# A scatter by GpSimd made to follow the projections of a spiking attention and mixture-of-experts layer, step by step

## The reference

```python
xn = layernorm(x)
# attention: spikes are 0/1, lif(v, th) = (v >= th)
Q = lif(layer_norm(xn @ Wq.T + bq, gq, betaq), 1.0)   # K and V likewise, 16 heads of 16
attn = Dh - hamming(Q, K) + log_position_bias          # no softmax
out = lif((attn * scale) @ V, 0.5)
attention = lif(layer_norm(out @ Wo.T + bo, go, betao), 1.0)
# experts: 8 experts, the two best for each token
probs = softmax(xn @ router_w.T); scores, idx = top_k(probs, 2); scores /= scores.sum()
hidden_e = silu(h_e[:, :256]) * h_e[:, 256:],  h_e = xn @ up_proj[e]
experts = sum over the two chosen e of score_e * (hidden_e @ down_proj[e])
```

## Time and profile before

| What | Value |
|---|---|
| Three runs, median | 511.02 us (509.71, 511.02, 511.58) |
| The profiled execution, span from first to last instruction | 510.6 us |
| TensorE busy in it | 384.5 us, 75% |
| VectorE, ScalarE, GpSimd busy | 273.3, 232.6, 211.0 us |
| Mean granted TensorE clock | 0.883 |
| Bytes moved | 58.98 MB, mean 116 GB/s |

### The profile page before, as it was taken

The page is one execution under the profiler, slowest core; times in us unless marked ns, Lnnn a source line. Parts: engine busy times, 40 slices in busy tenths (PEclk is TensorE's granted clock), DMA queues, the critical chain, the costliest instruction groups (busy, mean ns, idle before and its releaser), DMA issues.

```text
span 510.6 us, 9171 instructions
## 1 busy us (share of the span) xinstructions
PE 384.5 (75%) x2517; PEld 312.9 (61%) x2526; DVE 273.3 (54%) x774; ACT 232.6 (46%) x752; POOL 211.0 (41%) x213
## 2 busy tenths in 40 slices
PE   5498773110113999998999999999999999999960
PEld 2234662100112999997778888888888887667650
DVE  5799971000100687996545444554455442458995
ACT  1567421000001788986545544454445543366650
POOL 5242467777771000000233333333333333259993
PEclk9799985555555799999999999999999999999995
DMA  8721223222220111320443344343443332495222
GB/s 269 247 96 41 83 83 125 104 104 104 104 105 31 42 41 41 106 83 1 144 131 121 121 119 136 118 124 113 124 134 123 118 98 74 184 369 193 100 84 83
DMA packets 40432, 58.98 MB, mean 116 GB/s; under 512 B 6294, under 2 KB 27926, under 8 KB 40408
## 3 DMA queue, kind: packets, MB, share of 16 engines
q1 hardware_dynamic: 31712, 38.53, 24.5%
q0 software_dynamic: 6848, 18.70, 10.1%
q10 hardware_dynamic: 1848, 1.47, 0.9%
HBM read 35.79 MB, written 22.89 MB: 115 GB/s over the span
## 4 chain that ended last, share of the span: by engine, by line
PE 54%; issue 21%; DVE 10%; POOL 7%; DMA 3%; ACT 2%; SPq 1%; POOLq 0%; DVEq 0%; ACTq 0%
PE bank L1108 15%; PE bank L1109 14%; PE bank L1110 14%; POOL xres L718 3%; PE bank L1186 3%; PE bank L1251 3%; POOL xres L711 3%; PE bank L1235 3%; DMA xn<-x 2%; DVE xn L787 2%; DVE xst L765 2%; POOL rstd L703 1%; DVE w_f L808 1%; PE bank L1174 1%; PE bank L1195 1%
## 5 line engine op out<-in xcount | busy, mean ns | idle before, releaser
L692 POOL DMA_INDIRECT slot_y<-ey,dest x71 | 68.5, 965 | 214.6 <-ACT ey L554 186.2
L500 ACT ACTIVATE junk<-bank 128x256 bf16<-128x256 f32 x96 | 35.7, 379 | 89.8 <-remote 71.7
L677 POOL DMA_INDIRECT slot_x<-xn,pos x64 | 61.6, 963 | 23.9 <-issue 19.2
L996 DVE TENSOR_TENSOR hid<-gact,bank 128x256 f32<-128x256 f32 x71 | 29.9, 421 | 76.6 <-ACT gact L538 51.0
L1108 PE MATMUL bank<-ew,exT_h 128*128 x142 | 62.6, 441 | 5.6 <-issue 4.3
L1110 PE MATMUL bank<-w_h,xT_l 128*128 128x256 f32 x192 | 56.9, 296 | 11.3 <-issue 11.2
L795 DVE TENSOR_TENSOR xT_l<-xT,xT_h 128x256 fp32r<-128x256 f32 x28 | 12.9, 460 | 98.1 <-issue 54.1
L1109 PE MATMUL bank<-w_l,xT_h 128*128 128x256 f32 x192 | 56.9, 296 | 11.2 <-issue 11.2
L1108 PE MATMUL bank<-w_h,xT_h 128*128 128x256 f32 x192 | 57.1, 297 | 10.5 <-issue 10.4
L538 ACT ACTIVATE gact<-bank 128x256 f32<-128x256 f32 x71 | 27.4, 386 | 63.8 <-PE bank L1110 63.8
L1110 PE MATMUL bank<-ew,exT_l 128*128 x142 | 55.9, 394 | 0.0
(11 more groups left out here) (193 smaller groups left out, 967.9 us busy)
## 6 DMA issues: line engine op xcount, KB each, us to landing
ex<-slot_x SPq DMA_DIRECT2D x71, 129.0 KB
y_tok<-slot_y SPq DMA_DIRECT2D x8, 1024.0 KB, 13.6
ew_f<-experts SPq DMA_DIRECT2D x24, 256.0 KB, 2.6
xres<-x SPq DMA_DIRECT2D x16, 256.0 KB, 2.8
out<-xres SPq DMA_DIRECT2D x16, 256.0 KB, 2.1
xn<-x SPq DMA_DIRECT2D x6, 512.0 KB, 11.7
slot_y<-ey,dest POOLq DMA_INDIRECT x71, 2.8
xn<-x SPq DMA_DIRECT2D x4, 256.0 KB, 3.8
```

The source lines that it names most:

```text
L500: nc.scalar.activation(junk[:, i, :], proj_ps[r][i], ACT.Square, accum_out=ssq[:, r, i:i + 1]).then_inc(s["ssq_done"], 1)
L677: pool.indirect_dma_start(slot_x, bass.IndirectOffsetOnAxis(ap=pos[:, k, t:t + 1], axis=0), xn[:, t, :], None).then_inc(s["scattered"], 16)
L692: pool.indirect_dma_start(slot_y, bass.IndirectOffsetOnAxis(ap=dest[:, m % 4:m % 4 + 1], axis=0), ey[:, m % 4, :], None).then_inc(y_out[m ...
L996: v.tensor_tensor(hid[:, m % 2, :], gact[:, m % 2, :], h_ps[m % 2][:, F:2 * F], ALU.mult).then_inc(s["hid_done"], 1)
```

## The change

POOL waits before the two scatters of tile t until `proj_done` is at 3(t+3), that is, until the projections of step t+2 are done. Tiles 30 and 31 have no wait of their own and follow tile 29, which waits for the last step, 31.

```diff
 LAG = 3
 LATE = 11
+LEAD = 3
 FAR_ROWS = 5
...
             pool.wait_ge(s["placed"], 1)
             for t in range(NT):
+                if t + LEAD <= NT:
+                    pool.wait_ge(s["proj_done"], G3 * (t + LEAD))
                 for k in range(TOPK):
                     pool.indirect_dma_start(slot_x, bass.IndirectOffsetOnAxis(ap=pos[:, k, t:t + 1], axis=0),
                                             xn[:, t, :], None).then_inc(s["scattered"], 16)
```

## The result

The changed kernel takes 453.88 us (median of 4 runs, 452.99 to 455.22), the kernel before, run beside it, 511.23 us. The ratio is 0.888, with a 95% interval of 0.885 to 0.890. The forecast was 446, with a range of 431 to 487.

The account below looks back on a forecast made before the run. TensorE sets the pace except in a hole from about 77 to 166 us, blamed on dense scatters. From 510.6, projections ending at 162 instead of 235.3, plus 9 for the tail, gave 446.3, said as 446, range 431 to 487 us.

Parts of the forecast that it names:

- The hole and its cause: TensorE nearly idle from about 77 to 166 us because dense scatters hold back its issue and signals; at most 86 to 87 us to gain.
- Why the change helps: The scatter stream stays nearly as dense but now stops when TensorE falls behind; the hole was possible because POOL never stopped.
- Loss in the steps: 26 projection steps after step 5, at 2.9 us plus a chosen 0.5 us loss each, 13 us; projections end at 162.
- The tail: Last scatters and the `ex` load after step 31 delay the experts: 10.4 us less about 1.5, set at +9, bounds +7 and +11.
- some of it comes back: Last q turns, spikes and k-v sums run in the wait for the first `ex`, returning about 1.5 us.
- The pads' wait of ScalarE: ScalarE's step 11 needs tile 6's pads, queued behind POOL's new wait: 1 to 2 us once, hidden if POOL keeps up.
- The signs: Expected trace: scatters spread to about 168, ScalarE's remote waits under 15 us, first `ex` turn 10 to 13 us after projections.
- short falls: TensorE's granted clock, PEclk, was to stay near 1.0 apart from brief drops.
- 1, exclusion: Scatter and projection exclude each other however issued: projections end at 231, total 515; chance 0.06 in full or nearly.
- 2, an aftermath of each pair: The held-back state outlasts each tile's two scatters, 10 us each: steps of 12.5 us, total 683; chance 0.05.
- 3, written-out instructions: The hole belongs to the written-out code of steps 5 to 7 and stays; only the tail is added: 520; chance 0.04.
- 4, scatters only while VectorE is idle: Scatters proceed only when VectorE is idle: 4.4 us each, steps of 8.9 us, total 589; chance 0.01.

Follow-up runs that it names:

- 21, then a pause: Kernel before, but tiles 7 and up wait for all projections, so 21 transfers run first and 50 after: 511.98 us, ratio 1.000.
- halves of 64 rows: Kernel before, with each row scatter of 128 rows made as two of 64 rows, result the same: 599.57 us, ratio 1.172.
- At 1.43 us: Kernel before, no wait for projections; GpSimd does one small memset, waited for, after each of 71 transfers: 495.87 us, ratio 0.968.
- the kernel with two memsets: Kernel before, no wait for projections; two small memsets, each waited for, after every transfer (pitch 1.65 us): 464.80 us, ratio 0.908.
- a lead of 5: Changed kernel with LEAD 5 in place of 3, so tile t's scatters wait for step t+4: 461.62 us, ratio 0.903.
- The kernel with the new order: Changed kernel with the last spikes, q turns and k-v sums ahead of the first expert tile on TensorE, VectorE, ScalarE: 452.68 us, ratio 0.885.

## Why the prediction came out as it did

**The hole and its cause (right, and now shown).** The reading was that a dense stream of transfers holds back what TensorE issues and signals. Spreading it out takes the hole away, stopping it ends the hole, and nearly twice as many transfers make it nearly twice as long. (Two slips in the reading don't touch this: the hole's slices start with a 3 that the reading left out, and the 71.7 us are the three waits before `junk`, 8.0, 34.9, and 28.8; the 8.3 before `qT` come on top.) The runs add the size of it. Take the time from the first transfer to TensorE's last gap that is put down to `issue`, and divide it by the number of transfers:

| kernel | transfers | pitch, us | from the first to the last such gap, us | per transfer |
|---|---|---|---|---|
| before | 71 | 1.27 | 65.5 to 165.3 | 1.41 |
| 21, then a pause | 21 | 1.27 | 65.5 to 95.05 | 1.41 |
| halves of 64 rows | 135 | 1.21 | 67.6 to 254.8 | 1.39 |

The three agree at about 1.4 us. It is tempting to read this as the time for which each transfer keeps something busy that TensorE needs too, so that at a pitch of 1.27 a backlog of 0.14 us is added with each. Two runs speak against that simple form. At 1.43 us no backlog should grow, and the hole was still there, with 216 matmuls in 90 us. And 50 transfers at 1.27 us with TensorE idle should have left 50 × 0.14 = 7 us, and left none. So the 1.4 us hold for transfers and TensorE's work together, and are no price of a transfer by itself: transfers and TensorE seem to share something, and when the transfers come every 1.27 to 1.43 us there is not enough left for TensorE, whose work is then late and outlasts them. This is argued from the two runs, not shown. At 1.65 no loss is seen. Bytes and rows don't enter, nor whether the steps are written out. What the shared thing is, the runs don't show.

**Why the change helps (half right).** I had written that the hole was possible because GpSimd never stopped. The tie to TensorE does stop it, 17 times, but the kernel with two memsets shows that no tie is needed, only distance; and with the tie the order is free, ahead or behind. With the wait the mean pitch came out at 1.51 us, with stops just where TensorE is late. An even pitch of 1.51 without the tie was not run, so how much is the pitch and how much the place of the stops stays open.

**Loss in the steps (right in the sum, partly by luck).** Forecast: projections' end at 162, that is 73.3 us earlier. Measured: 72.1. Step 5 ends at 73.6 in the trace of after too, and 26 steps to 163.2 are 3.45 us each, forecast 2.9 + 0.5 = 3.4. The two parts were off against each other: the undisturbed step is 2.74, the loss 0.7. My 2.9 was 70 us over 24 steps, with the recovery of step 8 in it, and the 0.5 was a choice between bounds that no row set. The loss is uneven. The steps 7 to 10 (76.8 to 99.0) take 22.2 us, 11.2 more than 4 × 2.74, and lose more than half of the 18 us in all. They lie beside the seven pads (76.5 to 93.3), which have no wait of their own. With a lead of 5 the pads move to 82.8 to 99.8, and there the slow steps are those from 82.7 to 107.1; the last of these, 8.8 us from 98.4 on, has ScalarE's wait for the pads in it. That the pads cause the rest fits both traces, and no run took them away.

**The tail (the mis-sized term).** Forecast: +9, from 10.4 gross less 1.5. Measured: +10.7 gross, right to 0.3, then nothing back and 2.0 more, +12.7 in all. The step that failed is "some of it comes back: the last q turns, spikes and k-v sums, which now lie between the first expert tiles, can run in the wait". VectorE's program has `exT_l` of the first expert tile ahead of the last `qk_spk`. It waits 13.28 us for it at 176.56 and does the spikes at 177.58, behind the wait and not in it. The kernel with the new order does them at 167.00 and gets 1.4 us back, close to that credit. A part of the rest may be the clock: after the idle time the granted clock is 0.63 on average in the 10 us from 175, where 0.5 is the level of 1.2 GHz, and the first four `ex` turns take 1.21 us from first to last in place of 0.61; how much of the 2.0 us that explains wasn't measured. Against the span, 446.3 forecast and 451.2 measured, 3.7 of the 4.9 us are this term and 1.2 the steps. Of the other 2.7 to the median, 1.8 are what a run's time has over its span, which the forecast left out, and 0.9 lie between the profiled execution and the median run.

**The pads' wait of ScalarE.** Set at 1 to 2 us or hidden. In the changed kernel no such wait shows among ScalarE's large ones. With a lead of 5 ScalarE stands idle for 5.7 us before 102.9, at the place of this wait, and with two memsets for 12.4 us.

**The signs (all but one came).** L680 spreads to 170.6 (forecast 168), with L1113 as its releaser; "remote" of ScalarE is 10.5 (under 15); the clock stays near 1 but for the dips; the `ex` turn comes 12.5 us after the last projection (10 to 13); the end is within 3 us of 273.8. PEclk falls to 0.84 at 77 to 99 us, longer than "short falls" said.

**The rivals.** 1, exclusion: refuted by 647 matmuls beside 59 transfers, and by 16.0 of 16 us in the kernel with two memsets. 2, an aftermath of each pair: there is an aftermath, but it grows with the number of transfers and with TensorE's work beside them, and none is left at a distance of 1.65. 3, written-out instructions: refuted by that same kernel, and by the held steps 8 to 14 at 1.43. 4, scatters only while VectorE is idle: the median is 961 ns with VectorE busy for 58 of 90 us, as it was with 4.4. But the median hides something: the mean rose from 963 to 994 ns, and eight of the 64 took 1.03 to 1.47 us. Apart from the first, at 65.0, all of these started while a VectorE instruction with both inputs in SBUF was running, and took longer by what was left of it, less 0.12 us:

```profile
102.28 0.68 DVE L940 TENSOR_TENSOR ew<-ew_f,ew 128x512 f32 x1
...
102.42 1.37 POOL L680 DMA_INDIRECT slot_x<-xn,pos  x1 [1.03 <-PE bank L1113]
```

```profile
151.76 0.68 DVE L940 TENSOR_TENSOR ew<-ew_f,ew 128x512 fp32r<-128x512 f32 x1
151.81 1.47 POOL L680 DMA_INDIRECT slot_x<-xn,pos  x1 [0.31 <-issue]
```

The transfers that started inside the spikes (L963), which take one input from TensorE's result in `bank`, took at most 0.97 us. The Trainium skill, page "SBUF — State Buffer", section "Who interferes with whom", says that a VectorE instruction with two SBUF inputs contends with a GpSimd instruction that reads SBUF; these rows agree. It cost GpSimd about 2 us in all, far from the 4.4 us for each transfer of rival 4.

## What to carry to other kernels

When an engine shows long idle times as "issue", or its consumers wait on "remote" for matmuls recorded long ago, look at what GpSimd issues meanwhile: not its bytes, but transfers per microsecond. In this kernel an even distance of 1.27 or 1.43 us between indirect transfers held TensorE back, and 1.65 did not; with a wait on TensorE's progress a mean of 1.51 was enough. So try such a wait first, or other work between the transfers, start the stream as early as its data allow, and save transfers before saving bytes. When an early load loses its cover, move the work that could fill the wait ahead of it on every engine's queue, or it won't be done there.

## What the runs showed of the hardware

Signals can come long after the record of their instruction: the matmul recorded at 73.35 released ScalarE at 123.97, 50 us later. An indirect transfer of 128 rows takes GpSimd 0.96 us with 8 bytes a row and with 1032, one of 64 rows 0.90 us, and TensorE beside a dense stream was held for about 1.4 us for each of either kind. A stream as dense beside an idle TensorE left nothing behind. Two memsets of 0.16 us after each transfer, waited for, turned a loss of almost all of TensorE's time to none that shows. A transfer that starts inside a VectorE instruction with two SBUF inputs takes longer by the rest of that instruction less 0.12 us. While held back, the starts of TensorE's matmuls lie at multiples of about 0.70 us (2.80, 2.10, and 3.50 in the kernel with halves, from 233.09 to 249.89, after the last transfer); why, no run shows.
